# Flamingo block on one core: P weighed four units behind its scores, and the orders of the front and the tail rewritten

## The reference, cut to what matters

```
x += tanh(g) * (quant(ln(x)) @ quant(ctx))                       # 8 bit values, scores without a softmax
x += tanh(g) * (ln(x) @ W.T + b + low-rank terms made by an inverse real Fourier transform)
q = ln(x) @ Wq.T; k, v = [ctx, ln(x)] @ Wk.T, Wv.T               # 16 heads of 96, 4 kv heads, 1536 keys
x += tanh(g) * (softmax(q @ k.T / sqrt(96)) @ v) @ Wo.T
w, i = top_k(softmax(ln(x) @ Wr.T + br), 8)                      # 64 experts
x += tanh(g) * (ln(x) * sum(w) + scatter(w, i) @ expert_bias)
```

## Time and profile before

| | us |
|---|---|
| median of 3 runs | 1069.95 (1069.88 to 1073.51) |
| the profiled execution | 1068.31, of it span 1066.5 |
| PE busy | 1039.7 (97%) |
| DVE, ACT, POOL busy | 640.3, 636.0, 644.9 (60% each) |
| granted TensorE clock, mean of the span | 0.991 of full speed |

### The profile page before, as it was taken

One profiled execution on the slowest core, in us unless ns is written; L12 is line 12 of the kernel. 1 busy time (PEld: TensorE's weight loads), 2 busy tenths in 40 slices (PEclk: granted clock), 3 DMA queues, 4 the chain that ended last, 5 costly groups with the idle time before them and its releaser, 6 DMA issues.

```text
span 1066.5 us, 18352 instructions
## 1 busy us (share of the span) xinstructions
PE 1039.7 (97%) x7242; PEld 586.9 (55%) x7242; DVE 640.3 (60%) x1092; ACT 636.0 (60%) x711; POOL 644.9 (60%) x348
## 2 busy tenths in 40 slices
PE   9999999999999999999999999999999999989886
PEld 4555444444545565556656656656665665655552
DVE  6889859644124565555565655655655655576666
ACT  5786535431224687656667756666765666677843
POOL 4476889142001589665668855758866567688851
PEclk9999999999999999999999999999999999999996
DMA  9987664842233999998999999999999899999993
GB/s 337 265 292 218 200 226 109 178 76 53 72 111 88 173 215 214 218 204 154 199 177 195 182 214 174 167 193 192 179 212 206 150 190 173 149 191 186 177 189 119
DMA packets 516426, 192.46 MB, mean 180 GB/s; under 512 B 484900, under 2 KB 500132, under 8 KB 516340
## 3 DMA queue, kind: packets, MB, share of 16 engines
q1 hardware_dynamic: 516340, 191.28, 86.9%
HBM read 56.88 MB, written 13.63 MB: 66 GB/s over the span
## 4 chain that ended last, share of the span: by engine, by line
PE 80%; POOL 8%; DMA 3%; DVE 3%; issue 3%; ACT 2%; SPq 1%; POOLq 0%; DVEq 0%; ACTq 0%
PE ps L552 27%; PE ps L792 20%; PE ps L766 11%; PE ps L807 10%; PE ps L809 5%; PE ps L693 3%; POOL p L1708 2%; POOL region_c L1708 2%; DMA region_o<-region_y 1%; DMA ln_t<-stage 1%; DVE p_max L1543 1%; POOL region_y L1708 1%; PE ps L574 1%; POOL x_res L1708 1%; DMA stage<-ctx_t_in 1%
## 5 line engine op out<-in xcount | busy, mean ns | idle before, releaser
L1708 POOL TENSOR_TENSOR region_y<-p,region_b 128x1536 f16<-128x1536 f32 x128 | 396.9, 3101 | 273.7 <-ACT region_b L1244 255.6
L1234 ACT ACTIVATE p<-ps,p_max 128x1536 f32<-128x1536 f32 x128 | 197.2, 1541 | 199.8 <-DVE p_max L1543 199.5
L1543 DVE TENSOR_REDUCE p_max<-ps 128x1 f32<-128x1536 f32 x128 | 224.9, 1757 | 113.8 <-PE ps L792 113.8
L792 PE MATMUL ps<-region_q,region_c 96*128 96x512 f16 x1152 | 269.8, 379 | 0.0
L807 PE MATMUL ps<-region_q,region_c 128*128 128x192 f16 x1536 | 207.6, 246 | 5.1 <-DVE logit L1568 3.0
L1244 ACT ACTIVATE region_b<-ps,p_max 128x1536 f16<-128x1536 f32 x128 | 196.5, 1535 | 15.1 <-DMA region_c<-region_b 14.6
L809 PE MATMUL ps<-region_q,region_o 128*128 128x96 f16 x1536 | 202.3, 206 | 0.0
L792 PEld LDWEIGHTS ps<-region_q,region_c 96*128 96x128 f16 x1152 | 105.3, 98 | 108.0 <-ACT region_b L1244 0.9
L807 PEld LDWEIGHTS ps<-region_q,region_c 128*128 128x128 f16 x1536 | 150.2, 98 | 23.7 <-issue 5.0
L809 PEld LDWEIGHTS ps<-region_q,region_o 128*128 128x128 f16 x1536 | 150.3, 98 | 13.2
L552 PE MATMUL ps<-region_w,region_q 128*128 128x512 f16 x576 | 134.9, 379 | 2.3 <-DMA region_q<-region_q 1.7
(11 more groups left out here) (149 smaller groups left out, 1152.4 us busy)
## 6 DMA issues: line engine op xcount, KB each, us to landing
stage<-ctx_in SPq DMA_DIRECT2D x16, 512.0 KB, 5.1
stage<-ctx_t_in SPq DMA_DIRECT2D x15, 512.0 KB, 8.8
stage<-wq_in SPq DMA_DIRECT2D x16, 384.0 KB, 4.1
stage<-wo_in SPq DMA_DIRECT2D x16, 384.0 KB, 4.2
k_scratch<-region_o SPq DMA_DIRECT2D x12, 384.0 KB, 6.4
region_q<-k_scratch SPq DMA_DIRECT2D x8, 576.0 KB, 5.8
region_q<-v_scratch SPq DMA_DIRECT2D x8, 576.0 KB, 6.3
x_res<-x_in SPq DMA_DIRECT2D x8, 512.0 KB, 8.9
```

Of the source, the lines that this page charges most:

```text
L792: ins = nc.tensor.matmul(bank(NSB * (m % 2) + sb_), q_head[0:HD, b, h, hq, qt * P:(qt + 1) * P], k_head[0:HD, b, hk, sb_ * 512:(sb_ + 1) * ...
L1234: nc.scalar.activation(p32[:, m % 2, :], rows, ACT.Exp, bias=p_max[:, m % 4:m % 4 + 1], accum_out=den[:, m % 4:m % 4 + 1]).then_inc(e32_ok, 1)
L1543: nc.vector.reduce_max(p_max[:, m % 4:m % 4 + 1], rows, axis=AX, negate=True).then_inc(max_ok, 1)
L1708: return nc.gpsimd.tensor_tensor(out, a, b, op)
```

## The change

LAG becomes 4. The ring `den` grows to eight, as a row sum now lives a unit longer. The turn of o is done in front of the units with m % 4 = 0 and no longer 3. WO_AT stays as it is; WO_AT_LAST and the expert tables of the last task move on by one unit, and the mixture (2, 0) goes to the tail. The loads of K and V for the next task move from u = 1 to u = 4. q_product of the first queries waits for each piece of the split weights where one wait stood before it for all. fourier(4..7) stands before column_sums(1). The tail gets a new order on PE, DVE, ACT and POOL; `keep_busy(n)` adds n matmuls of 512 columns to a bank that nobody reads, 20 in all; and the last store is issued in two halves, each behind its own addition.

```diff
-LAG = 3
+LAG = 4
...
-        WO_AT_LAST = {1: 4, 2: 5, 5: 6, 6: 7, 9: 0, 10: 1, 13: 2, 14: 3}
+        WO_AT_LAST = {2: 4, 3: 5, 6: 6, 7: 7, 10: 0, 11: 1, 14: 2, 15: 3}
...
-        ROUTE = {2: 0, 4: 1, 7: 2, 11: 3, 15: 4}
+        ROUTE = {3: 0, 5: 1, 8: 2, 12: 3}
...
-            return (m - 7) // 4 if m >= 7 and m % 4 == 3 else None
+            return (m - 8) // 4 if m >= 8 and m % 4 == 0 else None
...
-                if u == 1 and 0 < t < TS - 1:
+                if u == 4 and 0 < t < TS - 1:
                     sp.wait_ge(pv_ok, UPS * t)
                     load_k(t + 1)
...
-            for i in range(3, NT):
+            for i in range(3, NT - 1):
                 store(i)
-            sp.wait_ge(out_st, 16 * NT)
+            for half in range(2):
+                hs = slice(half * 512, (half + 1) * 512)
+                sp.wait_ge(fin_ok, 2 * NT - 1 + half)
+                sp.dma_start(out_d[(NT - 1) * P:NT * P, hs], x_tile(NT - 1, half * 512, 512)).then_inc(out_st, 16)
+            sp.wait_ge(out_st, 16 * (NT + 1))
...
+            fourier(range(RING, NC))
             column_sums(1)
-            fourier(range(RING, NC))
...
+                    if part is None and j == 0 and c % 2 == 0 and n == 0:
+                        pe.wait_ge(w_split, W_WQ0 + c // 2 + 1)
...
-            pe.wait_ge(w_split, W_WQ0 + RING)
...
+            def keep_busy(n):
+
+                for _ in range(n):
+                    nc.tensor.matmul(bank(3), ones_h[:, :], eb_hi[:, 0:512], start=True, stop=True)
+
...
+            weigh(NU - 4)
             pe.wait_ge(exp_ok, NU - 1)
...
+            keep_busy(6)
             pe.wait_ge(fin_ok, 8)
             expert_mix(7, 4, 0)
             expert_mix(6, 4, 1)
-            expert_turn(4, 5)
...
+            expert_turn(4, 5)
+            keep_busy(3)
             pe.wait_ge(lg_step, 6)
             router(5, 6)
+            keep_busy(2)
...
+            keep_busy(9)
             pe.wait_ge(wx_ok, 6)
...
+            deviations(5, LN4)
             expert_low(5)
```

More of the change, by code:

```diff
@@ L279, in flamingo @@
         LAST = NU - UPS
-        STATS4 = {-2: 0, 0: 1, 3: 2, 7: 3, 11: 4, 15: 5}
-        NORM4 = {-1: 0, 1: 1, 4: 2, 8: 3, 12: 4}
-        LOW4 = {0: 0, 2: 1, 5: 2, 9: 3, 13: 4}
-        ROUTE = {2: 0, 4: 1, 7: 2, 11: 3, 15: 4}
[L284 to L289, removed]
+        STATS4 = {-2: 0, 0: 1, 4: 2, 8: 3, 12: 4}
+        NORM4 = {-1: 0, 1: 1, 5: 2, 9: 3, 13: 4}
+        LOW4 = {0: 0, 2: 1, 6: 2, 10: 3, 14: 4}
+        ROUTE = {3: 0, 5: 1, 8: 2, 12: 3}
+        CHOOSE = {4: 0, 6: 1, 9: 2, 13: 3}
+        CHOOSE_REST = {5: 0, 7: 1, 10: 2, 14: 3}
+        TURN_W = {6: 0, 9: 1, 11: 2, 15: 3}
+        SCALE_X = {6: 0, 9: 1, 11: 2, 15: 3}
+        MIX = {8: (0, 0), 9: (0, 1), 12: (1, 0), 13: (1, 1)}
+        STORE = {10: 0, 14: 1}
         def wo_n(g):
@@ L509, in _ @@
                 t, u = m // UPS, m % UPS
-                if o_at(m) is not None and m < NU - 1:
+                if o_at(m) is not None:
                     turn_o(o_at(m))
@@ L913, in _ @@
             out_last(1, 30, 0, (0, 1, 2))
-            out_last(2, 30, 1, (0, 1))
+            pe.wait_ge(fin_ok, 5)
+            expert_mix(7, 2, 1)
+            pe.wait_ge(exp_ok, NU)
+            router(5, 4)
             weigh(NU - 2)
-            out_last(2, 30, 1, (2,))
-            pe.wait_ge(exp_ok, NU)
-            expert_mix(5, 3, 0)
+            out_last(2, 30, 1, (0, 1, 2))
+            pe.wait_ge(fin_ok, 6)
+            expert_mix(7, 3, 0)
             pe.wait_ge(o_ok, NU - 1)
@@ L925, in _ @@
             turn_last(4, 31, (2,))
-            pe.wait_ge(fin_ok, 7)
+            pe.wait_ge(lg_step, 5)
             expert_turn(5, 4)
@@ L935, in _ @@
             router(5, 5)
+            pe.wait_ge(wo_free, 64)
+            keep_busy(6)
             pe.wait_ge(fin_ok, 8)
@@ L1267, in _ @@
             expert_norm(5)
+            expert_exp(4)
             take_last(2, 4, 31, slice(0, 2))
@@ L1661, in take_low_last @@
                       o_t[:, k % 2, HI, js, :]).then_inc(lt_lo, 1)
+            invert(NU - 4)
+            take_out(NU - 4)
+            add_mix(7, 2, 0)
+            expert_stats(5)
             take_low_last(1, 0, 30, slice(0, 3))
@@ L1665, in _ @@
             take_out(NU - 3)
+            add_out(1, 60)
             add_mix(7, 2, 1)
+            logits(5, 4)
             choose(4, 4)
-            add_out(1, 60)
             invert(NU - 2)
@@ L1675, in _ @@
             take_out(NU - 1)
+            expert_stats(6)
             take_low_last(3, 4, 31, slice(2, 3))
-            expert_stats(6)
             add_out(0, 62)
@@ L1779, in add_bias @@
                 pool.wait_ge(y2_ok, i + 1)
+                if i == 0:
+                    pool.wait_ge(cast_lo, 1)
                 tt(x_tile(i), x_tile(i), bias_rows, ALU.add).then_inc(xbias_ok, 1)
```

19 lines of the change are left out of this document (9 added, 10 removed).

## The result

Over seven runs of each, the changed kernel takes 1075.4 us (1072.51 to 1076.66), the kernel before 1070.19 (1068.85 to 1073.51): a ratio of 1.0041, 95% interval 1.0023 to 1.0059. Between the medians that is 5.2 us slower (4.4 by the ratio), where 3.5 were forecast. It is the forecast's own side, and its main mechanism, with several terms of another size. The profiled execution took 1076.66 us, at the upper end of its seven runs, and its span of 1074.8 is 8.3 longer than that of before.

The account below looks back on a forecast made before the run. PE was taken as the bound, attention's middle being one queue of matmuls without waits. Front −0.7, attention +5.4, tail −1.2 gave +3.5: 1071.8 us on the profiled run, 1073.4 with the median's offset; 8-in-10 range 1063 to 1080.

Parts of the forecast that it names:

- (f): Attention, task 0: turn 1 issued later, out_product at u = 14 waits 2.4, u = 2 of task 1 0.3: +2.7.
- (h): Expert steps one unit later: the first routers' waits on ln_t go, the others stay: −1.2 (−4 to +1).
- (a): Front: q_product waits for each piece of the split weights, so PE's wait for all four goes: −1.0.
- (d): Attention: one weighing and half of the last output product move behind the last scores: −3.4, back in the tail.
- (e): Attention, u = 2 at six task boundaries: turn of o one unit later lands late, out_product waits: +6.4.
- (i): Tail, last scores to the last weighing's end: 3.44 more PE work there, 20.5 for 17.8: +2.7.
- (j): Tail, last weighing to last addition: expert_stats off the chain −1.1, clock held for routers −1.0, mixing −1.4: −3.5.
- (k): Tail: last store in two halves, the first on its way when the last addition ends: −0.4 (−1 to +0.3).
- A: Rival in attention: the turns of o come in time, no waits for them: −9.1, 1064.3 us; chance 0.30.
- B: Rival in the tail: the clock falls all the same and fillers stand in the way: +5.4, 1078.8; chance 0.14.
- C: Rival in attention: turns land later than the median, sharing DMA queues with transposes and loads: +8, 1081.4; chance 0.09.
- D: Rival: no expert waits go, and ACT's rows cost 1.5 at the front: +2.4, 1075.8; 0.47 together with the forecast.

Follow-up runs that it names:

- last experiment: Kernel before with the change's front edits, 20 fillers and half stores, plus 8 thrown-away matmuls behind unit 4's router in the last task: 1065.46 us, 0.9962.

## Why the prediction came out as it did, step by step

The direction was right for the reason given: attention's middle had no idle time to win, and the turn of o moved past its slack. That the size came so near is in part luck: between the medians it is 5.2 us, but the two profiled runs are 8.3 apart, and in them (f) and (h) are 5.9 above the forecast. By the two profiles, in the order of the sum:

| step | forecast | measured | |
|---|---|---|---|
| front (a), (b) | −0.7 | −0.3 | start of the first scores, 333.83 to 333.50 |
| (c) unit 3 | +0.9 | +1.1 | units 3 and 4: 9.48 to 9.08, less the 1.5 of (d) |
| (f) turn 1, and task 1 | +2.7 | +6.0 | 5.2 at m = 14, 0.8 at u = 2 of task 1 |
| (e) u = 2 of tasks 2 to 7 | +6.4 | +4.6 | 0.5, 1.2, 0.5, 1.5, 0.5, 0.3 |
| (d) moved work | −3.4 | −3.4 | back in (i) |
| (h) expert waits | −1.2 | +1.4 | the last task's length, less (d)'s 1.9 and (e)'s last 0.3 |
| (i) to the last weighing | +2.7 | +2.4 | 17.8 to 20.2 |
| (j) to the last addition | −3.5 | −3.3 | 25.9 to 22.6 |
| (k) last store | −0.4 | +0.1 | 3.0 to 3.1 |
| sum | +3.5 | +8.6 | spans: +8.3, the rest small differences of other units |

(e) had the right issue (6.3 behind the unit's start) and too long a landing: 3.05 here and 3.1 in the median, for the 3.4 of before. Three boundaries of 0.5, one of 0.3 and two of 1.2 to 1.5 are the two kinds forecast. The experiment with the later products took this away and nothing else; the earlier turn took it away with the wait of (f).

(f) is the term that was most mis-sized. The turn's time was right (issued 406.45, landed 410.24; forecast 406.8 and 410.2), but PE came at 406.9 and not 407.8, and behind the wait of 3.5 the product ran at half clock, 1.7 more. (f) took both times from the old kernel, without the 1.3 us by which its own (a) to (d) move them; PE then came 0.9 sooner and the turn only 0.3. The half clock was nowhere in the sum.

(h) failed in sign. The waits did shift (ln_t <- stage from 2.0 to 1.3 in that stretch), but unit 5 has a router, a wait of 0.7 before it and one of 1.8 behind it, and then a weighing at 1.2 GHz: again the clock, 1.3 to 2 us. Since the clock can fall or stay behind such waits (last experiment), and stayed in the profile of before, part of this term belongs to the pair of profiles and not to the change.

The loads of K and V I costed at 0, and nothing here speaks against that number for where they stand. But it was argued from their own next use, and they matter through what stands behind them: one unit sooner they cost 7.7 us.

At the front PE is 0.25 us behind before the first edit (its waits at 125.31 and 125.06) and 0.33 ahead at the first scores, so the edits gave some 0.6 of the 0.7 forecast: two waits gone (1.0 and 0.8) and a new one behind DVE and ACT (1.1). That is less than the scatter between profiles.

(i) and (j) came out within 0.3, but (j) by terms that make up for each other. Taking expert_stats off the chain gave 1.3 (1.1 forecast). The routers gave none of their 1.0: from the start of expert_stats(6) to their end it takes 14.7 us, before 14.6, since the clock was at half again from 1058.9 and five fillers stood on the chain, 1.28 and 0.43 us. The stretch behind them, mixtures and additions, gave 2.1 for the 1.4 forecast (10.1 to 8.0). (k) gave nothing: a half store landed no sooner. The section of the Trainium skill that the forecast cites for (k) ("DMA: Bandwidth & Descriptors", Anatomy of one DMA) describes transfers issued by GpSimd, and this store is issued by SP. The profiled run stands above its median, as before's stood below its own; between the medians the sum is 5.2, between the profiles 8.3.

Of the rivals, A (turns in time) is out by the 9.7 us of waits, B as a whole by the clock of 0.86 and by the run without fillers, C by landings of 3.1. D's first half happened. Of B one part happened: the clock fell once, at 1058.9, among the transposes of block 7, and the fillers around the router stood on the chain. The transposes alone do not decide it. The same fillers, waits and transposes stand in the tails of six profiles (the changed kernel and five variants of it); in three the clock fell there (this one, the later products, the loads at u = 3), in three it stayed at 1.00 (the two with an early turn, the fillers in the wait).

## What to carry to other kernels

Where PE has no idle time, a longer software pipeline has nothing to win; ask instead which slack each moved step had, counted in units between its issue and its reader, and at the place with the shortest units, since that one decides. A small transfer behind big ones in the same queue pays for them in its landing (6.0 to 7.7 us here, where 3.1 is the median), so the order in a DMA queue belongs to the slack. And an idle time of two us or more on PE has to be priced with the half clock that may come behind it. Behind 3.2 to 3.7 us it came every time here, behind 1.7 to 2.6 not always. Twenty throw-away matmuls in the waits of the tail were the cheapest gain here: 3.6 us in the new order and, together with the front's edits and the half stores, 2.6 in the old.

## What the runs showed of the hardware that was not expected

After 3.47 us without a matmul the granted clock was 0.50 from 411 to 413 us, and nine matmuls of 512 columns took 3.77 us and not 2.11; with 14 matmuls thrown away in the wait it stayed at 1.00 and the product took 2.12. Without such matmuls it fell in all six profiles that have this wait, of 3.2 to 3.7 us. Shorter waits did not decide it. In the last task of the old attention with the new ends two waits of 0.55 and 1.99 us, with the 24 small matmuls of a router between them, were followed by the same fall (0.57 from 961 to 965), and so were 0.30 and 2.25 with the late turn; 0.21 and 2.33 in the kernel before, and 0.32 and 2.23 with the late turn and the late loads, were not. Single waits of 0.35 to 1.56 at u = 2 had no fall behind them in any profile; one of 1.75 there, in the profile with the fillers at m = 14, had (its product took 3.58). The length of the waits does not tell these apart, and what does stays open.

A DMA transpose of P issued behind 1.2 MB of loads held SP's queue for up to 4.4 us in the kernel before, 5.2 in the changed one and 5.7 with the late turn, where the median is 1.6 to 1.7. The small transpose of o, issued right behind such loads, landed in 6.0 to 7.7 us where the median is 3.1.
